# Attention scores of the first layer: three 64-row products in two row groups of TensorE instead of two stacked 128-row products

## What is computed

```python
x_norm = _group_norm(x, gn_scale, gn_bias).reshape(b, seq, c)
qkv = x_norm @ w_qkv + b_qkv
q, k, v = jnp.split(qkv, 3, axis=-1)          # 8 heads of 64 channels each
weight = jnp.einsum('bhld,bhsd->bhls', q * scale, k * scale)
weight = jax.nn.softmax(weight, axis=-1)      # 1024 x 1024 for each head
out = jnp.einsum('bhls,bhsd->bhld', weight, v)
out = out.transpose(0, 2, 1, 3).reshape(b, seq, c) @ w_out + b_out
return (x_flat + out).reshape(b, h, w, c)
```

## Time and profile before

| | us |
|---|---|
| median of three runs | 4447.74 (4446.66 to 4449.88) |
| span of the profiled execution, first to last instruction | 4446.7 |
| layer 0, to the last phase of its last image | 2424 |
| layer 1 | 2023 |
| attention of one image, from its first row maximum to its last | 180.5 |
| TensorE busy (matmul records), whole span | 4141.7 (93%) |
| VectorE, ScalarE, GpSimd busy | 3072.2, 2523.0, 1310.3 |

### The profile page before, as it was taken

The page is one execution under the profiler, slowest core; times in us unless marked ns, Lnnn a source line. Parts: engine busy times, 40 slices in busy tenths (PEclk is TensorE's granted clock), DMA queues, the critical chain, the costliest instruction groups (busy, mean ns, idle before and its releaser), DMA issues. The chain is left out here.

```text
span 4446.7 us, 65289 instructions
## 1 busy us (share of the span) xinstructions
PE 4141.7 (93%) x22762; PEld 3441.1 (77%) x22762; DVE 3072.2 (69%) x5125; ACT 2523.0 (57%) x5486; POOL 1310.3 (29%) x1423
## 2 busy tenths in 40 slices
PE   7999989989999899899898898989899998989999
PEld 6987978978879789789787577777777776777777
DVE  3983965948839749568397467686776857576867
ACT  3864846828738558368285255454546463535545
POOL 1432422423314224323243004040413222130404
PEclk9999999999999999999999899999999999999999
DMA  2221221211212212112121212030303031212212
GB/s 79 48 67 30 67 58 29 49 58 39 62 39 44 68 39 58 58 29 57 48 48 59 88 43 72 23 85 8 99 16 95 20 76 39 64 51 49 65 30 66
DMA packets 113184, 236.20 MB, mean 53 GB/s; under 512 B 17260, under 2 KB 33704, under 8 KB 112808
## 3 DMA queue, kind: packets, MB, share of 16 engines
q1 hardware_dynamic: 112808, 231.41, 19.5%
HBM read 80.35 MB, written 33.55 MB: 26 GB/s over the span
## 5 line engine op out<-in xcount | busy, mean ns | idle before, releaser
L560 DVE TENSOR_REDUCE a_neg_max<-a_ps 128x1 f32<-128x1024 f32 x512 | 626.0, 1224 | 396.3 <-PE a_ps L443 396.3
L519 ACT ACTIVATE a_ph<-a_ps 128x512 fp32r<-128x512 f32 x1024 | 555.0, 593 | 189.5 <-PE a_ps L454 186.4
L577 DVE TENSOR_TENSOR a_pl<-a_ps,a_ph 128x512 fp32r<-128x512 f32 x1024 | 654.5, 680 | 11.6 <-ACT a_ph L519 8.3
L526 ACT ACTIVATE a_prob<-a_ps,a_neg_max 128x1024 f32<-128x1024 f32 x512 | 572.7, 1119 | 20.5 <-DVE a_neg_max L560 20.5
L1545 POOL TENSOR_SCALAR b_prob<-b_prob,b_row_inv 128x256 f32<-128x256 f32 x512 | 245.6, 480 | 1091.3 <-DVE b_row_inv L1465 1055.5
L427 PE MATMUL a_ps<-a_ph,a_v 128*128 128x256 f32 x2048 | 550.7, 302 | 0.0
L640 POOL TENSOR_TENSOR a_qk<-a_fold_s,a_fold_r 64x256 f32<-64x256 f32 x256 | 188.2, 735 | 1213.2 <-DVE a_fold_s L568 1213.2
L454 PE MATMUL a_ps<-a_ident,a_prob 128*128 128x128 f32 x4096 | 534.4, 273 | 10.0 <-DVE a_pl L577 10.0
L454 PEld LDWEIGHTS a_ps<-a_ident,a_prob 128*128 128x128 f32 x4096 | 474.9, 140 | 86.7 <-issue 19.2
L427 PE MATMUL a_ps<-a_pl,a_v 128*128 128x256 f32 x2048 | 509.3, 282 | 0.0
L442 PE MATMUL a_ps<-a_kh,a_qs 128*128 128x512 f32 x1024 | 410.4, 401 | 31.1 <-ACT a_prob L526 13.0
(11 more groups left out here) (246 smaller groups left out, 9404.4 us busy)
## 6 DMA issues: line engine op xcount, KB each, us to landing
a_qs<-a_qk SPq DMA_DIRECT2D x128, 256.0 KB, 3.7
a_kl<-a_qk SPq DMA_DIRECT2D x128, 256.0 KB, 4.3
a_xtok<-in_x SPq DMA_DIRECT2D x64, 256.0 KB, 4.2
a_tok<-in_x SPq DMA_DIRECT2D x64, 256.0 KB, 4.3
x<-a_tok SPq DMA_DIRECT2D x64, 256.0 KB, 2.0
b_xs<-x SPq DMA_DIRECT2D x64, 256.0 KB, 4.3
b_qs<-b_qh SPq DMA_DIRECT2D x64, 256.0 KB, 3.0
b_qs<-b_ql SPq DMA_DIRECT2D x64, 256.0 KB, 3.8
```

Of the source, the lines that this page charges most:

```text
L519: act.activation(ph[:, b % 2, 4 * g:4 * g + 4, (u % 2) * P:(u % 2 + 1) * P], ps[:, 4 + n % 2, :].rearrange("p (k q) -> p k q", k=4), ACT.C ...
L526: act.activation(prob[:, i_ % 2, :], ps[:, 2 * (i_ % 2):2 * (i_ % 2) + 2, :] .rearrange("p a b -> p (a b)"), ACT.Exp, bias=neg_max[:, i_:i ...
L560: dve.tensor_reduce(neg_max[:, i_:i_ + 1], ps[:, 2 * (i_ % 2):2 * (i_ % 2) + 2, :] .rearrange("p a b -> p (a b)"), AX, ALU.max, negate=Tru ...
L577: dve.tensor_tensor(pl[here], ps[:, 4 + n % 2, :].rearrange("p (k q) -> p k q", k=4), raw(ph[here]), ALU.subtract).then_inc(pl_ok, 1)
```

## The change

The two terms are no longer stacked in one product. `qh` and `ql` hold the high and low part of q, each in both halves of the partitions. `kh` and `kl` now hold keys 0 to 511 in partitions 0 to 63 and keys 512 to 1023 in partitions 64 to 127. A step's scores are three products (`qh` with `kh`, `qh` with `kl`, `ql` with `kh`), each as two matmuls of 64 rows, one in each half of TensorE's rows, and each half writes its own PSUM bank. Low times low is left out.

```diff
-        qs = R.take("a_qs", [P, 2, TOK], F32R)
-        kh = R.take("a_kh", [P, 2, TOK], F32R)
-        kl = R.take("a_kl", [P, 2, TOK], F32R)
+        qh = R.take("a_qh", [P, 2, TOK], F32R)
+        ql = R.take("a_ql", [P, 2, TOK], F32R)
+        kh = R.take("a_kh", [P, 2, HALF], F32R)
+        kl = R.take("a_kl", [P, 2, HALF], F32R)
...
-        STAGE = 5
+        STAGE = 4
...
                             rows_ = slice(HD * half, HD * half + HD)
-                            sp.dma_start(raw(qs[rows_, j, :]), qk[own_half(h), p, :]).then_inc(s_ld[j], 16)
-                            sp.dma_start(raw(kl[rows_, j, :]), qk[own_half(h), CT + p, :]).then_inc(s_ld[j], 16)
+                            keys = slice(HALF * half, HALF * half + HALF)
+                            sp.dma_start(raw(ql[rows_, j, :]), qk[own_half(h), p, :]).then_inc(s_ld[j], 16)
+                            sp.dma_start(raw(kl[rows_, j, :]), qk[own_half(h), CT + p, keys]).then_inc(s_ld[j], 16)
...
-                            for kb in range(2):
-                                bank = ps[:, 2 * (i_ % 2) + kb, :]
-                                q_ = qs[:, j, t * P:(t + 1) * P]
-                                n = slice(kb * 512, (kb + 1) * 512)
-                                pe.matmul(bank, q_, kh[:, j, n], start=True, stop=False)
-                                mm = pe.matmul(bank, q_, kl[:, j, n], start=False, stop=True)
+                            n = slice(t * P, (t + 1) * P)
+                            for e, (a, b) in enumerate(((qh, kh), (qh, kl), (ql, kh))):
+                                for kb in range(2):
+                                    rows_ = slice(HD * kb, HD * kb + HD)
+                                    mm = pe.matmul(ps[:, 2 * (i_ % 2) + kb, :], a[rows_, j, n], b[rows_, j, :],
+                                                   start=e == 0, stop=e == 2)
                             mm.then_inc(score, 1)
```

More of the change, by code:

```diff
@@ L615, in stage @@
                         j, n = h % 2, STAGE * h
-                        hi = kh[:, j, :]
                         if 0 in parts:
                             pool.wait_ge(s_ld[j], 64 * (h // 2 + 1))
-                            pool.tensor_scalar(hi, raw(qs[:, j, :]), 1.0, 0.0, ALU.mult, ALU.add).then_inc(staged, 1)
+                            pool.tensor_scalar(qh[:, j, :], raw(ql[:, j, :]), 1.0, 0.0, ALU.mult, ALU.add)\
+                                .then_inc(staged, 1)
                             pool.wait_ge(staged, n + 1)
-                            pool.tensor_tensor(qs[HD:P, j, :], raw(qs[HD:P, j, :]), raw(hi[HD:P, :]), ALU.subtract)\
+                        if 1 in parts:
+                            pool.tensor_tensor(ql[:, j, :], raw(ql[:, j, :]), raw(qh[:, j, :]), ALU.subtract)\
                                 .then_inc(staged, 1)
                             pool.wait_ge(staged, n + 2)
-                        if 1 in parts:
-                            pool.tensor_scalar(qs[0:HD, j, :], raw(hi[0:HD, :]), 1.0, 0.0, ALU.mult, ALU.add)\
+                        if 2 in parts:
+                            pool.tensor_scalar(kh[:, j, :], raw(kl[:, j, :]), 1.0, 0.0, ALU.mult, ALU.add)\
                                 .then_inc(staged, 1)
                             pool.wait_ge(staged, n + 3)
-                            pool.tensor_scalar(hi, raw(kl[:, j, :]), 1.0, 0.0, ALU.mult, ALU.add).then_inc(staged, 1)
+                            pool.tensor_tensor(kl[:, j, :], raw(kl[:, j, :]), raw(kh[:, j, :]), ALU.subtract)\
+                                .then_inc(staged, 1)
                             pool.wait_ge(staged, n + 4)
-                        if 2 in parts:
-                            pool.tensor_tensor(kl[:, j, :], raw(kl[:, j, :]), raw(hi), ALU.subtract).then_inc(staged, 1)
-                            pool.wait_ge(staged, n + 5)
                     stage(0, (0, 1, 2))
```

## The result

The changed kernel is slower: 4478.43 us (4472.26 to 4481.71, four runs) against 4448.62 us (4446.66 to 4449.88, four runs), a ratio of 1.0062 with a 95% interval of 1.005 to 1.0075. That is little, but the two ranges don't touch. The forecast was 4360 us. The span of its profiled execution is 4476.0 us, 29.3 more than before.

What follows compares the result with a forecast made beforehand. TensorE was taken to bound the 59 full steps at 2.916 us. 2.86 - 0.93 + 0.78, plus 0.02 for splitting, gives 2.73; saving 0.186 x 59 x 8 = 88 us gives 4360 us, range 4332 to 4575.

Steps and rivals of the forecast that it cites:

- What bounds the kernel: Layer 0's 59 full steps an image: TensorE bounds each at 2.916 us; VectorE would at 2.65.
- Scores: Score matmuls of a step: three side-by-side pairs at 0.233 us take 0.70 us, with their loads hidden, instead of 0.93.
- one behind the other: Rival on the scores: halves don't run side by side, block 1.40 us, step 3.33, time 4643 us; chance 0.12.
- the loads no longer hide: Rival on score weight loads: each pair takes 0.34 us, block 1.02, step 2.95, time 4464 us; chance 0.08.
- Going to half rows and back: Switches around a step's scores: 0.08 us charged once, nothing on the way back; bounds nothing to 0.54 us.
- The array empties at every switch: Rival on TensorE's switches: 0.27 us each, block 1.24, step 3.17, time 4568 us; chance 0.20.
- The splitting: GpSimd's last part before a head: subtraction priced 1.29 to 1.55 us, leaving 0.02 us of wait a step.
- VectorE: Same work, 2.65 us a step, the cover that runs out; at free switching it would stop the gain at 126 us.
- Transfers: The two transfers of k become half as long, issued at the same places; nothing hangs on them.
- layer 1: The layer that isn't edited: should take the same 2023 us.

Runs made afterwards that it cites:

- the kernel with one half: Changed kernel with all six score matmuls on the lower half of TensorE's rows: 4853.23 us, ratio 1.0904.
- the pair of small matmuls: Kernel before plus two 64-column matmuls a step ahead of the scores, one on each half of the rows: 4621.17 us; both on all 128 rows: 4540.67 us.
- the second group of a step: Changed kernel with a step's first score pair ahead of the first four transposes and the other two pairs behind them: 4759.16 us, ratio 1.0684.

## Why the prediction was wrong

**What bounds the kernel** was right: TensorE in the 59 full steps, and a change of the step time times 472 gives the result.

**Scores** was right. Three pairs at 0.23 take the 0.70 us that I charged, and the loads are hidden inside the group. The rival "one behind the other" is refuted by the kernel with one half, and "the loads no longer hide" by the spacing of 0.23 between pairs: it is true only at the edge, for the second pair (0.34). The Trainium skill ("TensorE: Matmul & The Clock Gate", Part 3) has the sentence that loads overlap matmuls only in another row group. The traces differ from it, and the measurement decides: in the kernel with one half every load goes to rows that a matmul is using, and behind the first two the matmuls still start 0.23 apart.

**Going to half rows and back** is the step that failed. I charged 0.08 us once, with the reason that on the way back the transposes are paced by their own loads. They are, but only from the second one on. The trace after has: 0.21 for 0.12 into the first pair, 0.34 for 0.23 to the second, 0.33 for 0.23 out of the last, and 1430.62 - 1429.70 = 0.92 for 0.87 over the transposes. Together 0.09 + 0.11 + 0.10 + 0.05 = 0.35 us a step; the pair of small matmuls gives 0.29 to 0.31, the second group of a step 0.33. I had put the break-even at 0.28. With 0.35 the prediction's own sum is 2.86 - 0.93 + 0.70 + 0.35 = 2.98, and 2.978 was measured. So the rest of the sum stood and this one term decided. It lies between the two rows that I had as bounds, 0.08 once and 0.54; I took the lower because the spacings around today's scores are the usual ones. They are, but no row there has a change in the rows used, so they said nothing.

**The array empties at every switch** is the rival that came nearest: both switches cost, 0.17 each on the mean, not the 0.27 of a whole tail and a load. The time, 4478, lies in its interval of 4447 to 4570, to which I gave 0.20. That the number lies there proves little, since "the loads no longer hide" had 4464; the spacings and the experiments decide between them. The page "TensorEngine Tiling (Array Packing)" of the Trainium skill, Key Properties, says that changing the tiling mode drains the engine. The runs agree that such a change costs time; the page gives no number, and here a round trip took 0.29 to 0.35 us. What the time goes into is shown in part only. That the load behind a switch isn't hidden is seen in the 0.34; the 0.05 over the transposes lies between the first and the second of them, where the second's load is in the open too. The other 0.19, about 0.09 at the start of a group and 0.10 at its end, fits an array that has to empty, but no run shows that it does.

**The splitting** was better than charged: 1.29 us for the subtraction, the lower of my two prices, and no wait is left where I kept 0.02 us a step. That gave back 0.05 a step, 24 us by the sum and 19 by the kernel before with earlier splitting. Without this gain the change would have cost some 50 us and not 30.

**VectorE** kept its 2.65 us of work a step (156.04 / 59) and was never reached. I had expected TensorE to wait for `exp_ok` instead; it doesn't, since it stayed the slower of the two. **Transfers** and **layer 1** did nothing that counts: layer 1's first product (L922, then L923) starts 27.2 us later, and the span ends 29.3 later.

## What to carry to other kernels

Row groups are worth what they save between two switches, less a price for the pair of switches: here three pairs instead of four full matmuls save 0.23 us and the switches cost 0.35; with six pairs instead of eight the saving is 0.46 and it pays. So count the switches as well as the matmuls, and if no row of the trace has the switch, measure its price first with a small matmul pair on half rows against the same on full rows. Ask also what else a moved group waits for: with two groups a step, 0.21 us of wait came on top of the switches. When an edit changes two things, such as the products and the splitting that feeds them, look for the one that gains and apply it alone: here moving the splitting earlier gained 0.4%.

## What was not expected of the hardware

The order in which the program writes matmuls for the two halves of the rows didn't matter: with three on the lower half ahead of three on the upper one, pairs from both halves started within 0.01 us of each other, and the time was that of the interleaved order (4481.55 and 4478.43 us). Who exchanged them is not shown. And a switch between full rows and half rows cost about 0.3 us for the round trip, more than a score matmul of 512 columns (0.23 us).
